# A two-layer graph network on one core: bf16 row parts, bias additions and mixing moved between stages, gelu after the transpose, ranged semaphore clears

## The reference

```python
# layer 0: 8 heads of 32
h = (xn @ W.T).reshape(n, 8, 32)
enc = relu(edge_attr @ edge_W.T + edge_b).reshape(-1, 8, 32)
alpha = a_src . h[src] + a_dst . h[dst] + sum(enc * h[dst], -1)
alpha = where(alpha >= 0, alpha, 0.2 * alpha)
attn = softmax of alpha over the edges of each dst
x = x + segment_sum(h[src] * attn, dst) + bias + linear_attention(xn) @ wo.T + bo
x = x + experts_8(layernorm(x))
# layer 1: two graph attentions in a row, self loops added; first 4 heads of 128, then 1 head of 256
g = gelu(gat_conv(xn, W1, heads=4) + b1)
x = x + gat_conv(g, W2, heads=1) + b2 + linear_attention(xn) @ W_out.T + b_out
x = x + experts_32(layernorm(x))        # logits = rows @ router_w.T + router_b, argmax, two matmuls with relu
```

## Time and profile before

| | us |
|---|---|
| time, median of 3 runs | 3324.52 (3322.86 to 3326.3) |
| profiled execution | 3343.32 |
| its span | 3341.8, mean granted clock of TensorE 0.798 |

### The profile page before, as it was taken

One profiled execution on the slowest core, in us unless ns is written; L12 is line 12 of the kernel. 1 busy time (PEld: TensorE's weight loads), 2 busy tenths in 40 slices (PEclk: granted clock), 3 DMA queues, 4 the chain that ended last, 5 costly groups with the idle time before them and its releaser, 6 DMA issues. The chain is left out here.

```text
span 3341.8 us, 49981 instructions
## 1 busy us (share of the span) xinstructions
PE 2227.2 (67%) x10992; PEld 1501.8 (45%) x10993; DVE 2100.4 (63%) x3786; ACT 1244.8 (37%) x3566; POOL 1813.1 (54%) x1829
## 2 busy tenths in 40 slices
PE   3624778756997389948672999997523667654693
PEld 2222333334555356525561777775412444433351
DVE  7466877787888343352676788888744566565121
ACT  3214333325775221234001676774003667621010
POOL 1576777766554201133545777773576777751213
PEclk9866977777999599979675999998556999876555
DMA  4766888864885278826994888885885555510444
GB/s 140 198 185 193 263 261 258 265 214 116 219 217 162 101 256 272 261 87 209 374 390 159 269 275 282 280 269 123 294 261 154 147 149 148 145 43 13 131 151 130
DMA packets 456331, 673.50 MB, mean 202 GB/s; under 512 B 66642, under 2 KB 333324, under 8 KB 455617
## 3 DMA queue, kind: packets, MB, share of 16 engines
q1 hardware_dynamic: 333633, 358.22, 34.8%
q0 software_dynamic: 87248, 263.43, 26.6%
q10 hardware_dynamic: 35296, 50.06, 4.2%
HBM read 495.11 MB, written 177.80 MB: 201 GB/s over the span
## 5 line engine op out<-in xcount | busy, mean ns | idle before, releaser
L1474 POOL DMA_INDIRECT xn<-table,src_col x572 | 589.4, 1030 | 181.5 <-issue 161.1
L1515 PE MATMUL sum_h_ps<-xn,sum_h_hot 128*128 128x261 f32 (+1 forms) x1936 | 525.4, 415 | 194.0 <-DVE xn L1529 147.9
L1515 PEld LDWEIGHTS sum_h_ps<-xn,sum_h_hot 128*128 128x128 f32 x1936 | 369.7, 201 | 341.9 <-DVE xn L1529 248.8
L1051 POOL DMA_INDIRECT arena_a<-table,src_col x264 | 269.5, 1021 | 274.7 <-issue 203.2
L910 POOL DMA_INDIRECT arena_b<-table,src_col x336 | 326.7, 972 | 119.6 <-issue 97.9
L1529 DVE TENSOR_TENSOR xn<-xn,al 128x514 f32<-128x514 f32 (+1 forms) x352 | 243.9, 693 | 160.2 <-DMA xn<-table,src_col 153.9
L1538 DVE TENSOR_TENSOR arena_a<-arena_a,sum_h_ps 128x522 f32 (+1 forms) x440 | 246.4, 560 | 62.6 <-issue 42.4
L1648 PE MATMUL sum_ps<-xn,sum_hot 128*128 128x264 f32 x880 | 245.8, 406 | 31.9 <-DVE arena_a L1671 10.5
L933 PE MATMUL score_ps_hd<-arena_a,score_hot 128*128 x1320 | 234.4, 326 | 0.0
L943 ACT ACTIVATE xn<-score_ps_en 128x512 f32<-128x512 f32 x220 | 131.5, 598 | 274.0 <-PE score_ps_en L929 274.0
L1631 POOL TENSOR_TENSOR xn<-xn,al 128x264 f32<-128x264 f32 x220 | 156.7, 714 | 120.8 <-DMA xn<-edge_h 118.1
(11 more groups left out here) (511 smaller groups left out, 4776.3 us busy)
## 6 DMA issues: line engine op xcount, KB each, us to landing
xn<-edge_h SPq DMA_DIRECT2D x220, 264.0 KB, 3.2
edge_h<-arena_b SPq DMA_DIRECT2D x84, 528.0 KB, 4.6
arena_b<-kept SPq DMA_DIRECT2D x66, 516.0 KB, 5.5
xn_t<-edge_rows SPq DMA_DIRECT2D x110, 256.0 KB, 4.6
score_h_hot<-hots SPq DMA_DIRECT2D x220, 128.0 KB, 13.3
kept<-arena_a ACTq DMA_DIRECT2D x40, 516.0 KB
xn<-kept SPq DMA_DIRECT2D x66, 257.0 KB, 2.9
arena_a<-in_f_w SPq DMA_DIRECT2D x16, 1024.0 KB, 8.8
```

The costliest lines, as they stand in the source:

```text
L1051: pool.indirect_dma_start(rows[:, q, s, :], None, table, bass.IndirectOffsetOnAxis(ap=K.src_col[:, w * SUB + s:w * SUB + s + 1], axis=0)). ...
L1474: pool.indirect_dma_start(rows[w][:, s, 0:RW], None, table, bass.IndirectOffsetOnAxis(ap=K.src_col[:, w * SUB + s:w * SUB + s + 1], axis=0 ...
L1515: ins = pe.matmul(ps[:, u, b, 0:part], lhsT=hot[:, w % QH, s, :], rhs=rows[w][:, s, b * part:(b + 1) * part], start=(s == 0), stop=(s == S ...
```

## The change

Six edits. (1) `clear_stale` sorts the numbers of the semaphores and clears each run of neighbouring numbers with one instruction. (2) The roundings, subtractions and splits of the layer-0 rows and the encoder weights move from the head of `edge_scores_l0` into `linear_attention_l0`, behind DVE's last copy and ACT's last root there; POOL and PE of `edge_scores_l0` no longer wait for them. The bias addition to x moves from `segment_softmax` to the DVE of `linear_attention_l0`, one chunk in each wait for the square. (3) In `segment_softmax` the scans by head become one scan over H x (C + 1) elements and a copy; the mixing result is added to x by DVE after the last subtraction. (4) The layer-1 biases and mixing move from `finish_route_l1` to the end of DVE's and PE's lists in the one-head `edge_scores_l1`. (5) `middle_l1` transposes before the gelu: DVE forms f1 * acc + u2 in four fused operations, PE transposes that, and ACT takes the gelu from PSUM in four activations whose bias, b1, now lies along the partitions. (6) `finish_route_l1` keeps only two fused multiply-adds for each tile.

The diff, cut:

```diff
     def clear_stale(self, pool):
-        for s in self.stale:
-            pool.sem_clear(s)
+        numbers = sorted(s.num for s in self.stale)
+        first = 0
+        for n in range(1, len(numbers) + 1):
+            if n == len(numbers) or numbers[n] != numbers[n - 1] + 1:
+                pool.sem_clear(range(numbers[first], numbers[n - 1] + 1))
+                first = n
...
 def linear_attention_l0(prog, K, A):
...
+            sp.dma_start(enc_w[:, :], A["g0_enc"]).then_inc(s_encw, 16)
+            load_rows(sp, s_bias, bias[:, 0, :], A["g0_b"])
+            load_rows(sp, s_bias, bias[:, 1, :], A["m0_bo"])
...
+            act.wait_ge(s_c, 1)
+            for u in range(NT // U):
+                t = slice(u * U, (u + 1) * U)
+                act.activation(by_head[0][:, t], feats[:, t], ACT.Copy).then_inc(s_round, 1)
+            for u in range(4):
+                middle(u)
+            low(0)
+            middle(4)
+            for u in range(1, 5):
+                low(u)
...
+            step(dve.tensor_tensor(bias[:, 0, :], bias[:, 0, :], bias[:, 1, :], ALU.add))
             for c in range(NT // U):
...
                 dve.tensor_tensor(part, part, gmean[:, :].unsqueeze(2).broadcast_to([P, groups, MD]), ALU.subtract).then_inc(s_cen, 1)
+                x_c = K.x[:, c * U:(c + 1) * U, :]
+                ins = dve.tensor_tensor(x_c, x_c, bias[:, 0, :].unsqueeze(1).broadcast_to([P, U, D]), ALU.add)
...
             dve.tensor_copy(K.mix[:, :, :], ps_c[:, :, 0:D]).then_inc(s_kvos, 1)
...
+            for u in range(4):
+                upper(u)
+            lower(0)
+            lower(1)
+            dve.wait_ge(s_low, 1)
+            upper(4)
+            for u in range(2, 5):
+                lower(u)
+            split3(step, [near_h[c][:, :, :, DH0] for c in range(3)], K.att_n[:, :, H0:2 * H0], [rest[:, :, :]] * 2)
...
 def edge_scores_l0
...
-            sp.dma_start(pen, bass.AP(tensor=K.pen.tensor, offset=0, ap=[[L, C], [0, H], [1, L + 1]])).then_inc(s_pen, 16)
             for g in range(Q):
                 load(g)
+            sp.dma_start(pen, bass.AP(tensor=K.pen.tensor, offset=0, ap=[[L, C], [0, H], [1, L + 1]])).then_inc(s_pen, 16)
...
-            pool.wait_ge(s_rest, NT // U)
...
-            pe.wait_ge(s_terms, SPLITS0)
-            pe.wait_ge(s_round, 3 * (NT // U))
...
 def edge_scores_l1, one head: PE, then DVE
...
+            for t in range(NT if H == 1 else 0):
+                if t >= 2:
+                    pe.wait_ge(s_mixed, t - 1)
+                for k in range(2):
+                    ins = pe.matmul(mix_at[t % 2], lhsT=K.xn_t[:, k, t * P:(t + 1) * P], rhs=K.mix[:, k, :], start=(k == 0), stop=(k == 1))
+                ins.then_inc(s_mix, 1)
...
+                for c in range(NT // U):
+                    t = slice(c * U, (c + 1) * U)
+                    ins = dve.tensor_tensor(K.x[:, t, :], K.x[:, t, :], bias[:, 0, :].unsqueeze(1).broadcast_to([P, U, D]), ALU.add)
...
+                for t in range(NT):
+                    dve.wait_ge(s_mix, t + 1)
+                    dve.tensor_tensor(K.x[:, t, :], K.x[:, t, :], mix_at[t % 2], ALU.add).then_inc(s_mixed, 1)
...
 def segment_softmax: POOL, then DVE
...
-                    pool.tensor_tensor(K.x[:, t, :], K.x[:, t, :], bias[:, 0, :].unsqueeze(1).broadcast_to([P, U, D]), ALU.add).then_inc(s_biased, 1)
...
-                        pool.tensor_tensor(x_view[:, k, t, :], x_view[:, k, t, :], mix_out[:, k, t, :], ALU.add)
...
-                for h in range(H):
-                    ins = dve.tensor_tensor_scan(carry_row[:, d, 1:C + 1, h][:, order], ends_row[:, d, 1, :, h][:, order],
-                                                 ends_row[:, d, 0, :, h][:, order], -BIG, ALU.add, ALU.max)
...
+                step(dve.tensor_tensor_scan(lane[:, order], flat[1], flat[0], -BIG, ALU.add, ALU.max))
+                dve.tensor_copy(carry_row[:, d, d:d + C + 1, :].rearrange("p c h -> p h c"),
+                                lane[:, :].rearrange("p (h c) -> p h c", h=H)).then_inc(s_carry, 1)
...
+                    dve.wait_ge(s_mixed, (c + 1) * U)
+                    ins = dve.tensor_tensor(x_view[:, t, :, :], x_view[:, t, :, :], mix_out[:, t, :, :], ALU.add)
...
 def middle_l1
...
-            load_rows(sp, s_w, b1, A["g1_b1"])
+            sp.dma_start(b1[:, :], A["g1_b1"].rearrange("a (k p) -> p (a k)", p=P), allow_slow_non_contiguous=True).then_inc(s_w, 16)
...
-                    ins = pe.transpose(ps_g[:, t % 2, k * P:(k + 1) * P], g[:, t % 2, k * P:(k + 1) * P], K.ident[:, :])
+                    ins = pe.transpose(ps_g[:, t % 2, k * P:(k + 1) * P], u1[:, t % 2, k * P:(k + 1) * P], K.ident[:, :])
...
+                for k in range(4):
+                    ins = act.activation(g_t[:, t % 2, k, :], ps_g[:, t % 2, k * P:(k + 1) * P], ACT.Gelu, bias=b1[:, k:k + 1])
...
+                for h in range(H1):
+                    ins = dve.scalar_tensor_tensor(u1[:, t % 2, h * DH1:(h + 1) * DH1], acc[:, t, h * R:h * R + DH1], f1[:, t, h:h + 1],
+                                                   u2[:, t % 2, h * DH1:(h + 1) * DH1], ALU.mult, ALU.add)
...
 def finish_route_l1
...
-            for t in range(U + 2):
-                mix(t)
...
+                for t in range(c * U, (c + 1) * U):
+                    ins = dve.scalar_tensor_tensor(K.x[:, t, :], acc[:, t, 0:D], f1[:, t, 0:1], K.x[:, t, :], ALU.mult, ALU.add)
+                step(ins)
+                for t in range(c * U, (c + 1) * U):
+                    ins = dve.scalar_tensor_tensor(K.x[:, t, :], K.tab2[:, t, 0:D], f2[:, t, 0:1], K.x[:, t, :], ALU.mult, ALU.add)
+                step(ins)
```

More of the change, by code:

```diff
@@ L54 @@
 ENC_ROWS = 3 * (3 * 3 + 1)
-SPLITS0 = 2 * 5 + 7
 WSP = 448
@@ L665, in early_terms, with near_parts @@
     return K.al[:, WS * H0:WS * H0 + fits * n], K.arena_a[:, far:far + (EARLY0 - fits) * n]
+def near_parts(K):
+    near = K.arena_a[:, 0:NT * 3 * (D + H0) // 2].bitcast(BF16).rearrange("p (t c d) -> p t c d", t=NT, c=3)
+    return near, [near[:, :, c, :].rearrange("p t (h r) -> p t h r", h=H0) for c in range(3)]
 def linear_attention_l0(prog, K, A):
@@ L691, in linear_attention_l0 @@
         kvo = st.sbuf("kvo", [P, 2, D])
+        R = ENC_ROWS
+        near_h = near_parts(K)[1]
+        by_head = [part[:, :, :, 0:DH0] for part in near_h]
+        feats = K.tab0[:, :, :].rearrange("p t (h r) -> p t h r", h=H0)[:, :, :, 0:DH0]
+        home = NT * 3 * (D + H0) // 2
+        temps = [flat[:, n * U * D:(n + 1) * U * D] for n in range(2)] + [K.arena_a[:, home + n * U * D:home + (n + 1) * U * D] for n in range(2)]
+        temps = [temp.rearrange("p (t h d) -> p t h d", t=U, h=H0) for temp in temps]
+        enc_w = st.sbuf("enc_w", [R, D])
+        enc_rest = st.sbuf("enc_rest", [R, D])
+        enc_parts = st.sbuf("enc_parts", [R, 3, D], BF16)
+        part_is = st.sbuf("part_is", [R, 3])
+        rest = st.sbuf("rest", [P, NT, H0])
+        s_encw, s_round, s_rest, s_lower, s_low = (st.sem(n) for n in ("encw", "round", "rest", "lower", "low"))
         ps_kv = st.psum("ps_kv", [P, 4, 512])
@@ L828, in edge_scores_l0 @@
         al = K.al[:, 0:WS * H].rearrange("p (s h) -> p s h", h=H)
-        near = K.arena_a[:, 0:NT * 3 * (D + H) // 2].bitcast(BF16).rearrange("p (t c d) -> p t c d", t=NT, c=3)
-        near_h = [near[:, :, c, :].rearrange("p t (h r) -> p t h r", h=H) for c in range(3)]
+        near = near_parts(K)[0]
         flat = K.xn[:, :, :].rearrange("p t d -> p (t d)")
@@ L848, in edge_scores_l0 @@
         s_gath, gathered = K.gath, list(K.gathered)
-        s_hot, s_fin, s_copied, s_one, s_terms, s_encw, s_en, s_hd, s_enc, s_prod, s_red = (
-            st.sem(n) for n in ("hot", "fin", "copied", "one", "terms", "encw", "en", "hd", "enc", "prod", "red"))
-        s_round, s_rest = st.sem("round"), st.sem("rest")
+        s_hot, s_fin, s_copied, s_one, s_en, s_hd, s_enc, s_prod, s_red = (
+            st.sem(n) for n in ("hot", "fin", "copied", "one", "en", "hd", "enc", "prod", "red"))
         s_kept = [st.sem(f"kept{q}") for q in range(QR)]
-        h = K.tab0[:, :, :].rearrange("p t (h r) -> p t h r", h=H)[:, :, :, 0:DH0]
-        by_head = [near_h[c][:, :, :, 0:DH0] for c in range(3)]
-        h_rest = flat[:, 0:NT * D].rearrange("p (t h d) -> p t h d", t=NT, h=H)
         turns = W // (G * Q)
@@ L1069, in count_gathered, with edge_scores_l1 @@
         K.gathered[q] += 16 * SUB * len(range(q, n, Q))
-def edge_scores_l1(prog, K, name, H, C, RW, table, kept):
+def edge_scores_l1(prog, K, name, H, C, RW, table, kept, A):
     with Stage(prog, name) as st:
@@ L1111, in edge_scores_l1 @@
         s_pen = st.sem("pen")
+        if H == 1:
+            bias = K.al[:, 2048:2048 + 2 * D].rearrange("p (a d) -> p a d", a=2)
+            mix_at = (ps_t[:, 0:D], ps_n[:, 1, 0:D])
+            s_bias, s_biased, s_mix, s_mixed = (st.sem(n) for n in ("bias", "biased", "mix", "mixed"))
         block = st.block()
@@ L1115, in _ @@
         def _(sp):
```

(20 more changed lines are left out.)

157 lines of the change are left out of this document (62 added, 95 removed).

## The result

The changed kernel takes 3243.29 us (median of 4, 3241.79 to 3244.72) where the one before takes 3325.41 on the same chip: a ratio of 0.9742, with a 95% interval of 0.9724 to 0.9759. Beside new runs of before on another chip it was 0.9753 (0.9732 to 0.9774; 3253.56 to 3335.95). The forecast was 3236, in a range of 3216 to 3262.

The account below looks back on a forecast made before the run. No engine was taken as full: twenty barrier-closed stages, each bound by its own chain. Terms -8.5, -17.5, -10.3, +2.5, -10 and -45 sum to -88.8 us, giving 3235.7 on the median, forecast 3236, range 3216 to 3262.

Parts of the forecast that it names:

- Route, -45: Layer-1 route stage: ACT's 7.96 us per chunk becomes the bound, saving 45 us (40 to 50).
- Softmax 0, -17.5: Layer-0 softmax: POOL's additions go and one carry scan plus copy replaces scans by head, saving 17.5 us (14 to 20).
- Middle, -10: Middle of layer 1: PE or row loads replace DVE as pace, 25 x 0.45 us, saving 10 (5 to 13).
- Scores h1, +2.5: Layer-1 one-head edge scores: moved mixing is covered; only bias additions can block gathers, 1 to 7 us, taken as +2.5.
- Clears, -12.3: Heads of nine stages: single semaphore clears on POOL become ranged ones of 38 ns, saving 10.3 + 2.0 us.
- Rival C: Semaphore clears: a ranged clear costs per number as before, +12.3 us, so 3248; chance 0.10.
- Linear attention and edge scores 0, -8.5 with clears: Layer-0 rows moved: edge scores head saves 14.5 us, clears 2.0, held gathers in linear attention cost 8.
- the upper bound of the cost: Linear attention 0: the whole run of moved subtractions holds a gather, 13 us, from the gather at 275.71.
- Rival A: Gathers not held by moved work: linear attention 0 costs 1 us, score h1 0; -98, so 3226; chance 0.15.
- B: Gathers held for the whole run: 21 us instead of 8 and 7 instead of 2.5, so 3253; chance 0.15.
- D: Route and middle bound elsewhere, by PE at the lower clock or the loads: +10 to +20, 3251; chance 0.07.
- E: Slower than before: b1's 512 four-byte pieces move one after another and hold the middle's gelus; 3333 at 0.19 us each; chance 0.03.

Follow-up runs that it names:

- the slower chip: Chip of the first four follow-up runs, where the unchanged kernel before takes 3675.88 us; the route part alone against before has ratio 0.9968 there.
- the probe: Changed kernel plus ten idle DVE subtractions ahead of DVE's work in edge scores 0; first gather 1.71 us, the nine behind it 1.10.

## Why the prediction was right, point by point

**The time** fell in the range, 7 us above the forecast. Of the terms, route and softmax 0 were right in mechanism and size; the middle was right in size, with a part of its saving where I hadn't looked; the clears were put too large; and two were wrong in size in a way that cancelled. That the sum comes so close is partly luck: nothing made these two errors, 5.6 and 6.9 us, equal. The two profiles lie 101 us apart, 12 more than the sum, and the medians 82, 7 less.

- **Route, -45**: the profile pair gives 45.6 from the combination to the logits, as worked out from ACT's 7.96 per chunk (7.86 measured). The fused operation takes 0.41 us (2.07 for five) and not 0.35, so the first root comes at 6.9 instead of 6.2; DVE isn't the bound, and it costs only that.
- **Softmax 0, -17.5**: -17.8 by the stage, -18.3 alone. The carry scan was guessed at 0.3 + 0.15 and the copy at 0.4; they are 0.43 and 0.28. The terms as written add up to 17.1 and not 17.5, which is as near.
- **Middle, -10**: -11.6. PE became the bound at the 2.18 of the earlier trace rows, the value of the fast stretch, and the loads did not take over. But the 0.45 per tile came from no row (2.77 - 2.18 is 0.59): the average spacing went from 2.70 to 2.37, which is 8 us, and the other 3.7 is the first tile, whose transposes no longer wait for a gelu. The prediction had the start unchanged or later.
- **Scores h1, +2.5**: +3.4 with its clears unchanged, and 168.1 to 172.7 in five profiles with the clears, where kernels without the part have 166.2 to 167.6. The reason given (held gathers) is 0.75 of it, the rest sits in waits for stores. The mixing was priced at 42 us and takes 24. The cover that I called enough is enough only where gathers end the stage; the slower chip shows the price of losing it, 34 us, which I did not have among the rivals.
- **Clears, -12.3**: alone -7.0. The size that failed is that of the ranges left, 1.8 us in the eight stages instead of 0.4. One step failed too: that POOL's first gather heads sum h4's chain. It does start earlier, and then waits for the memset; the 12.44 us row was in the trace of before. But only 0.7 us hung on it, and with both corrected the term is -10.3; the rest up to -7.0 is inside the interval. Rival C (the old price per number) is out: with the clears alone a range of 10 numbers takes 0.088 us and one of 25 takes 0.174, some 0.006 for each number instead of 0.065.
- **Linear attention and edge scores 0, -8.5 with clears**: the net of the part was right (-6.5 without clears; -10.3, interval -5.7 to -15) from two wrong sizes. The cost for POOL was put at 8 and is 2.4: near the lower bound, one late hand-over, now understood as being in step with DVE's boundaries. The gain at the head of edge scores 0 was put at 14.5 and is 7.6, because 6 us of it was the single long gather. That same row had served as the upper bound of the cost, so one odd row pushed both terms, in opposite directions.

Rival A had the mechanism of the gathers right (hand-over at boundaries) but not its sum, since it kept the 14.5. B is out by the gathers of 1.10 us, D by transposes 2.18 and roots 7.86 apart, E by the earlier first transposes. The inference of the Trainium skill (SBUF — State Buffer, "Who interferes with whom") that tensor_tensor doesn't hold up descriptor generation isn't borne out: gathers of 2.42 us beside one of 2.88, and of 1.10 in step with those of 1.41, both show a wait, bounded by the instruction. A gather also reads its row numbers (`src_col`) from SBUF, and no run separates that read from the making of descriptors; what is shown is that the gather as a whole waits. The same section's "the other fully blocks", in the Trainium skill, holds here for each single instruction and not for a run of them.

The parts alone add up to -7.0 - 10.3 - 18.3 - 44.0, and -11.6 for the middle by its stage: -91, where the whole gives -82. Each has an interval of 4 to 8 us to either side, so this is no contradiction, but sum h4, which no part but the clears touches, is 442.7, 443.6 and 449.6 in the changed kernel (the second with the probe) and 440.1 to 440.9 in four of five profiles of before and its variants. Whether that is the missing part wasn't tested.

## What to carry to other kernels

Read a duration that carries a term from several instances or executions before it is used, above all where the same row bounds a cost and sizes a gain. Work moved into a stage is free only as long as the engine that ends that stage stays the same one: write down which it is, and by how much it would have to change (here PE fell behind on one chip, POOL no longer ended the stage, and 44 us turned into 12). A lower DMA rate over a longer stage with the same bytes explains nothing by itself; look at which engine is late and what it waits for. Before shortening what stands ahead of a gather, look at what the gather then waits for.

## What the runs showed of the hardware

- A DVE memset of 13050 f32 per partition, an even number, keeps a POOL gather from finishing until it ends: 12.28 to 13.76 us in all twelve profiles with it. One of 13049 elements takes the same 10.93 us and lets gathers run in 0.95, so it isn't the length. 13050 is the one even size that was tried; 6475, odd too, let four gathers run in 0.95.
- Gathers beside back-to-back two-input DVE operations of 1.41 us finish once per operation, some 0.9 us behind its boundary.
- Chips differ: with the same program and data, one chip agreed within 2.3 us in the stages bound by computation and took up to 1.43 times as long in those with gathers, loads and stores together. In scores h1 it was PE that fell behind there: 8 matmuls in 20 us amid the gathers, 208 after them, with 88 us of gaps before matmuls that wait for no semaphore, while POOL's gathers were as fast as elsewhere. The cause isn't known.
